# Two 32-column strips of TensorE by turns: the order of the head products in a decoder kernel

## The chip, the cores and the metric

The kernel runs on one core of a Trainium2 chip. The metric is the device time of one launch in microseconds (us). Three runs of the kernel before took 5780.36, 5787.46 and 5790.4 us; the median, 5787.46 us, is the time before.

## The reference

A decoder of four layers works on 32 sequences of 128 tokens with width 128. Each layer has a self-attention, a cross-attention over 77 context tokens and a feed-forward block, each followed by a sum and a layer norm, which makes twelve sublayers. Everything is float32. Three cross-attentions (those of the second, third and fourth layer, called L1X, L2X and L3X) and the self-attention of the fourth layer (L3A) share one form with 16 heads of width 8:

```python
q = split_heads(x @ Wq); k = split_heads(ctx @ Wk); v = split_heads(ctx @ Wv)
p = softmax(scale * q @ k.T + mask)        # 128 queries x 77 keys per head
o = merge_heads(p @ v)                     # 8 columns per head
y = o @ Wo
```

In L3A the keys are the 128 tokens themselves and a term of relative positions is added to the scores. The product p @ v is the one that the change touches.

## The kernel before

The 32 sequences are taken in four steps of eight. In a step the eight sequences are two groups g of four, and all twelve sublayers are done for them before the next step. Each engine has its own instruction list, written out by hand; they meet at semaphores. TensorE takes its list in the order in which it stands.

In L1X, L2X, L3X and L3A the work is cut into 16 units u. A unit is half of one sequence's heads: 8 heads, that is two blocks of 32 columns of the width (i = 0 and 1), each with four heads (r = 0 to 3). A unit passes these stages:

- scores (L1402 in the cross-attentions; L1995 and L1999 in L3A): TensorE multiplies the queries of a block, 32 rows of the array, by the keys, into PSUM banks 0 and 1 or 2 and 3. In L3A four transposes per bank put the position term there first.
- VectorE (DVE) takes the maximum and subtracts it (L1283 to L1292), ScalarE (ACT) takes the exponential (L1254), VectorE the sum and its reciprocal (L1299, L1301), GpSimd (POOL) multiplies (L1314).
- pe_probs_turn (L1222): TensorE transposes the eight 128 x 77 probability tiles into PSUM banks 4 and 5. ScalarE (L1261) and VectorE (L1308) copy them to the buffer PT, one bank each.
- pe_heads (L1239): the head products. The stationary operand is a 77 x 32 slice of v, in which only the 8 columns of head r are not zero; the moving operand is the turned probability tile of that head, 77 x 128. Four products, r = 0 to 3, add up in the 32 partitions c0 to c0+31 of PSUM bank 6 + g. Each product names its strip of the array by tile_position=(0, c0). Strip and target partitions differ between i = 0 and i = 1; the rows of the array are the same.

Each float32 product is two weight loads and two matmuls for TensorE, so the eight head products of a unit are 16 matmul records at L1239, called a burst below. A transpose is one record.

TensorE's list in such a sublayer is, for i from 0 to 18: scores(i), heads(i-3), turn(i-2). VectorE's is less_max(i), sums(i-1), copy of turned(i-2). At i = 5 TensorE also turns the second group's state and makes its queries (L159, L1377), at i = 12 it projects the first group's heads (L1247); at i = 13 and 14 VectorE sums and normalises the first group. Units 13 to 15 have no scores beside them any more.

Before a burst TensorE waits for both copies of the turned tiles. The last matmul of a burst raises c_pv, on which the copies of the next unit wait, and, at units 7 and 15, the copy of the heads.

The self-attention L1A has a head product of its own (L999), with 64-column strips. It already goes from one strip to the other with each product:

```python
for b in range(NB):
    for h in range(2):
        mm = nc.tensor.matmul(ps[64 * h:64 * h + 64, 4, b * P:(b + 1) * P], ...,
                              start=True, stop=True, tile_position=(0, 64 * h))
```

Of the kernel before, what the change touches and what calls it, by code (L numbers as in the profile page):

```python
# [56 lines left out]
def build(nc, dram, cols, out, steps):  # L57

    ctx = ExitStack()
    with ctx:  # L60
# [1165 lines left out]
        def pe_heads(pe, L, u):  # L1226
            m = CB[L]
            nk = m["nk"]
            j, half = divmod(u, 2)
            g, b = divmod(j, NB)  # L1230
            pe.wait_ge(c_ea.sem, c_ea[L, u])
            pe.wait_ge(c_ed.sem, c_ed[L, u])
            if u % 8 == 0:
                pe.wait_ge(c_vc.sem, c_vc[L, g])
                pe.wait_ge(c_qc.sem, c_qc[L, g])
            for i in range(2):
                c0 = 32 * (2 * half + i)
                for r in range(4):
                    mm = nc.tensor.matmul(ps[c0:c0 + 32, 6 + g, b * P:(b + 1) * P],  # L1239
                                          m["v"][g][0:nk, b, r, c0:c0 + 32], m["PT"][0:nk, 4 * i + r, :],  # L1240
                                          start=(r == 0), stop=(r == 3), tile_position=(0, c0))
            mm.then_inc(c_pv.sem, 1)
# [144 lines left out]
        def pe_context(L):  # L1387
            m = CB[L]

            def run(pe):  # L1390
# [18 lines left out]
                for i in range(16 + 3):  # L1409
                    if i == 5:  # L1410
                        pe_context_queries(pe, L, 1)
                    if i < 16:
                        scores(i)
                    if 0 <= i - 3:
                        pe_heads(pe, L, i - 3)
                    if 0 <= i - 2 < 16:
                        pe_probs_turn(pe, L, i - 2)
                    if i == 12:
                        pe_project_heads(pe, L, 0)
                    if i == 17 and L == L2X:  # L1420
                        pe_l2f_route(pe, 0)
                    if i == 16 and L == L1X:
                        pe_turn_state(pe, L1X, 0)
                    if i == 17 and L == L1X:
                        pe_l1f_gate_up(pe, 0)
# [531 lines left out]
        def pe_l3a(pe):  # L1957
# [45 lines left out]
            for i in range(16 + 3):  # L2003
                if i < 16:
                    scores(i)
                if 0 <= i - 3:
                    pe_heads(pe, L3A, i - 3)
                if 0 <= i - 2 < 16:
                    pe_probs_turn(pe, L3A, i - 2)
                if i == 12:  # L2010
                    pe_project_heads(pe, L3A, 0)
                if i == 16:
                    pe.wait_ge(c_sub.sem, c_sub[L3A, 15])
                    pe_context_part(pe, L3X, "k")
                if i == 17:
                    pe_context_queries(pe, L3X, 0)
                    pe_context_part(pe, L3X, "v")
# [776 lines left out]
```

## Time and profile before

| | |
|---|---|
| runs | 5780.36, 5787.46, 5790.4 us; median 5787.46 |
| span of the profiled execution | 5793.5 us |
| mean granted clock of TensorE | 0.836 of full speed |
| TensorE matmul busy | 4923.2 us, 85% of the span |
| VectorE busy | 2980.6 us, 51% |
| ScalarE busy | 1939.1 us, 33% |
| GpSimd busy | 1042.2 us, 18% |
| L1239 in the costliest groups | 353 us (w_even) as its largest part, 4096 matmul records in all |

The profile is of one execution. For it the span is the only time that is given; it lies 6 us above the median of the runs. PE is TensorE's matmul, PEld its weight load. A group is a line, an engine and an operation; "idle before" is the time in which the engine stood still just ahead of it, with the one that ended the wait. The granted clock is 1.0 at 2.4 GHz and 0.5 at 1.2 GHz. Matmul durations are those of single instructions, from start to end of their results; they overlap in the array, so a burst lasts much less than the sum of them. TensorE's busy time is the time in which at least one is under way.

### The profile page before, as it was taken

The numbers are of one execution on the slowest core, as the hardware profiler recorded it, in microseconds if no ns is written. First come the engines' busy times: TensorE is split into PE (matmuls) and PEld (weight loads), VectorE is DVE, ScalarE is ACT, GpSimd is POOL, SyncE is SP. The second block draws the span as 40 slices with busy tenths as digits, with TensorE's granted clock in tenths as the row PEclk, the third lists the DMA queues.
The fourth block names the chain that finished last, engine by engine and source line by source line (L and its number), as shares of the span: only waits on it lengthen the run. The fifth ranks groups of instructions, "written<-read, shape, count | busy, mean of one in ns | idle before, by whom it ended". The sixth has DMA issues, their size and how long they took to land. (4 is left out here: it accounts for less than half of the span.)

```text
span 5793.5 us, 57753 instructions
## 1 busy us (share of the span) xinstructions
PE 4923.2 (85%) x20360; PEld 2783.9 (48%) x20360; DVE 2980.6 (51%) x6224; ACT 1939.1 (33%) x3508; POOL 1042.2 (18%) x876
## 2 busy tenths in 40 slices
PE   6888899989688889998968888998886888899888
PEld 4445454653444545465344454445534455545553
DVE  5555443763555544376355554446535555534643
ACT  4242222336324222233632422222364242223235
POOL 2021100213202110021320211002222021100222
PEclk8896879969799777996879987898597998789869
DMA  2000100000100010000010001000001000100000
GB/s 75 1 3 24 52 5 2 1 16 0 51 1 3 24 52 5 2 1 15 0 51 1 3 24 52 5 2 16 1 1 50 1 3 24 52 5 2 16 1 4
DMA packets 20876, 93.08 MB, mean 16 GB/s; under 512 B 5228, under 2 KB 14444, under 8 KB 17796
## 3 DMA queue, kind: packets, MB, share of 16 engines
q1 hardware_dynamic: 20580, 89.26, 4.1%
q8 instruction: 170, 2.79, 0.2%
q14 instruction: 126, 1.03, 0.1%
HBM read 87.16 MB, written 2.10 MB: 15 GB/s over the span
## 5 line engine op out<-in xcount | busy, mean ns | idle before, releaser
L1314 POOL TENSOR_TENSOR arena<-arena 128x616 f32<-128x616 f32 (+1 forms) x256 | 355.0, 1387 | 1189.2 <-DVE arena L1301 1188.8
L1254 ACT ACTIVATE arena<-arena 128x616 f32<-128x616 f32 (+1 forms) x256 | 205.2, 802 | 930.7 <-DVE arena L1288 481.2
L1222 PE MATMUL ps<-const,arena 128*77 128x128 f32 (+1 forms) x2048 | 422.0, 373 | 69.1 <-POOL arena L1314 69.1
L210 POOL TENSOR_SCALAR rstd_e<-mean_var 128x4 f32<-128x4 f32 x120 | 27.4, 228 | 2467.8 <-DVE mean_var L176 2467.8
L1923 DVE TENSOR_TENSOR arena<-ps,arena 128x512 f32<-128x512 f32 x256 | 176.5, 691 | 468.7 <-ACT arena L1873 468.7
L1222 PEld LDWEIGHTS ps<-const,arena 128*77 128x77 f32 (+1 forms) x2048 | 340.1, 207 | 153.6 <-POOL arena L1314 82.2
L1239 PE MATMUL ps<-arena,w_even 77*32 77x128 f32 (+1 forms) x2560 | 352.9, 355 | 50.8 <-DVE arena L1308 50.4
L1873 ACT ACTIVATE arena<-ps 128x512 f32<-128x512 f32 x288 | 172.0, 597 | 607.9 <-PE ps L1821 607.9
L1239 PEld LDWEIGHTS ps<-arena,w_even 77*32 77x32 f32 (+1 forms) x2560 | 264.3, 141 | 190.8 <-ACT arena L1261 87.1
L2263 PE MATMUL ps<-w_even,w_odd 128*128 128x512 f32 x640 | 321.6, 649 | 26.9 <-issue 26.9
L1308 DVE COPY arena<-ps 77x512 f32<-77x512 f32 (+1 forms) x256 | 174.5, 682 | 270.2 <-PE ps L1222 270.1
L1820 PE MATMUL ps<-xT,w_even 128*128 128x512 f32 x576 | 308.9, 618 | 3.1 <-DVE arena L1910 3.1
L1827 PE MATMUL ps<-arena,w_even 128*128 128x512 f32 x576 | 295.0, 594 | 7.0 <-DVE arena L1923 4.7
L745 PE MATMUL ps<-xT,w_even 128*128 128x512 f32 (+1 forms) x544 | 269.2, 618 | 0.4
L1821 PE MATMUL ps<-arena,w_even 128*128 128x512 f32 x512 | 266.3, 602 | 0.0
L1261 ACT ACTIVATE arena<-ps 77x512 f32<-77x512 f32 (+1 forms) x256 | 151.0, 590 | 328.7 <-PE ps L1222 328.5
L1402 PE MATMUL ps<-arena 32*128 32x308 f32 x768 | 211.3, 663 | 41.8 <-DVE arena L1288 25.2
L199 DVE TENSOR_TENSOR y_tok<-ps,x_tok 128x512 f32<-128x512 f32 x72 | 49.4, 686 | 357.3 <-PE ps L683 265.5
L1299 DVE TENSOR_REDUCE arena<-arena 128x8 f32<-128x616 f32 (+1 forms) x256 | 228.2, 892 | 0.5
L1559 PE MATMUL ps<-arena,w_odd 128*128 128x512 f32 x512 | 220.4, 592 | 0.0
L2263 PEld LDWEIGHTS ps<-w_even,w_odd 128*128 128x128 f32 x640 | 125.2, 205 | 186.9 <-issue 179.2
L2467 DVE SCALAR_TENSOR_TENSOR arena<-ps,arena 128x512 f32<-128x512 f32 x48 | 33.2, 692 | 343.8 <-ACT arena L2352 342.9
(383 smaller groups left out, 9365.4 us busy)
## 6 DMA issues: line engine op xcount, KB each, us to landing
w_even<-in_w SPq DMA_DIRECT2D x4, 6916.0 KB, 19.2
w_even<-in_w SPq DMA_DIRECT2D x4, 3313.5 KB, 10.9
w_odd<-in_w SPq DMA_DIRECT2D x4, 2824.5 KB, 9.4
w_odd<-in_w SPq DMA_DIRECT2D x4, 2095.0 KB, 8.2
w_odd<-in_w SPq DMA_DIRECT2D x4, 2048.0 KB, 15.2
x_in<-in_x SPq DMA_DIRECT2D x10, 256.0 KB, 2.8
w_odd<-in_w SPq DMA_DIRECT2D x4, 577.0 KB, 3.6
w<-in_w SPq DMA_DIRECT2D x1, 2050.0 KB, 10.7
```

The costliest lines, as they stand in the source:

```text
L745: mm = nc.tensor.matmul(ps[0:rows, k + i % 2, :], lhsT, xT[g][:, :], start=True, stop=True)
L1222: mm = nc.tensor.transpose(ps[0:nk, 4 + h // 4, (h % 4) * P:(h % 4 + 1) * P], m["P"][u % 3][:, h, :], ident)
L1239: mm = nc.tensor.matmul(ps[c0:c0 + 32, 6 + g, b * P:(b + 1) * P], m["v"][g][0:nk, b, r, c0:c0 + 32], m["PT"][0:nk, 4 * i + r, :], start=(r ...
L1254: nc.scalar.activation(p, p, ACT.Exp, scale=scale).then_inc(c_exp.sem, 1)
L1299: nc.vector.tensor_reduce(m["sum"][u % 3], m["P"][u % 3], AX.X, ALU.add)
L1314: nc.gpsimd.tensor_tensor(m["P"][u % 3], m["P"][u % 3], bcast(m["sum"][u % 3], m["nk"]), ALU.mult)\
L1402: mm = nc.tensor.matmul(ps[:, 2 * (u % 2) + i, 0:4 * KC], m["q"][g][r:r + 32, b * P:(b + 1) * P], m["k"][g][r:r + 32, b, :, :], start=True ...
L1559: mm = nc.tensor.matmul(bank(4 + n % 2), W(L1F, w)[:, k * T + c * P:k * T + (c + 1) * P], src[g][:, k, :], start=(k == 0), stop=(k == 3))
L1820: nc.tensor.matmul(bank(i % 2), w1, xT[g][:, :], start=True, stop=True)
L1821: nc.tensor.matmul(bank(2 + i % 2), w3, x3, start=True, stop=True).then_inc(e_gu.sem, 1)
L1827: nc.tensor.matmul(bank(6 + g), w, e_h[i % 2], start=(n == 0), stop=(n == 35)).then_inc(e_down.sem, 1)
L2263: nc.tensor.matmul(o, W(L3F, "ew2")[:, p * 384 + m * P:p * 384 + (m + 1) * P], i_hm[g][4 * (j - 1) + p], start=(p == 0), stop=False)
```

## The change

In pe_heads the two loops are exchanged. Before, the four products of strip i = 0 are issued, then the four of strip i = 1. After, the products alternate: r = 0 of both strips, r = 1 of both, and so on. The number of products, their operands, the sums in each strip and their order, and the last instruction of the burst (r = 3 of i = 1) stay the same; L3A, L1X, L2X and L3X all call this function.

```diff
-            for i in range(2):
-                c0 = 32 * (2 * half + i)
-                for r in range(4):
+            for r in range(4):
+                for i in range(2):
+                    c0 = 32 * (2 * half + i)
                     mm = nc.tensor.matmul(ps[c0:c0 + 32, 6 + g, b * P:(b + 1) * P],
                                           m["v"][g][0:nk, b, r, c0:c0 + 32], m["PT"][0:nk, 4 * i + r, :],
                                           start=(r == 0), stop=(r == 3), tile_position=(0, c0))
```

TensorE's instructions in L1X, one turn of the loop, in its list; the eight products of a burst stand in one row, since a row names shapes and not partitions:

```order
L1402 MATMUL ps<-arena0 128x308 x2
L1239 MATMUL ps<-arena0,w_even 32x128 x8
L1222 MATMUL ps<-const,arena0 77x128 x8
L159 MATMUL ps<-const,x_tok1 128x128 x4
L1377 MATMUL ps<-xT1,w_even 128x512
```

These rows are the same before and after. What moves is inside the row of eight. With a for strip i = 0 and b for i = 1 it was a0 a1 a2 a3 b0 b1 b2 b3 and is a0 b0 a1 b1 a2 b2 a3 b3. The two rows L159 and L1377 stand in the turn i = 5 alone.

TensorE's instructions in L3A, one turn:

```order
L1995 MATMUL ps<-const,arena1 128x128 x4
L1999 MATMUL ps<-w_odd,w_even 128x512
L1995 MATMUL ps<-const,arena1 128x128 x4
L1999 MATMUL ps<-w_odd,w_even 128x512
L1239 MATMUL ps<-arena1,w_even 32x128 x8
L1222 MATMUL ps<-const,arena0 128x128 x8
```

Here too nothing moves but the order within the burst of L1239. The lists of the other engines and of the DMA queues are unchanged.

## Rows read from the trace of the kernel before

**Rows 1.** Page, parts 1 and 4: busy time, and the last-ending chain by engine and line.
```profile
PE 4923.2 (85%) x20360; PEld 2783.9 (48%) x20360; DVE 2980.6 (51%) x6224; ACT 1939.1 (33%) x3508; POOL 1042.2 (18%) x876
...
PE ps L1239 2%; PE ps L1222 1%; PE ps L745 1%; PE ps L2263 1%; PE ps L1402 1%; PE ps L1999 1%; PE ps L755 0%; PE ps L2215 0%; POOL rstd L212 0%; PE ps L974 0%; PE ps L949 0%; PE ps L999 0%; DVE x_tok L182 0%; PE ps L1007 0%; PE ps L1995 0%
```
**Rows 2.** Page, part 5: the copy ahead of the bursts (busy, mean ns | idle before).
```profile
L1308 DVE COPY arena<-ps 77x512 f32<-77x512 f32 (+1 forms) x256 | 174.5, 682 | 270.2 <-PE ps L1222 270.1
```
**Rows 3.** Timeline of PE, L1X of step 1: start us, us, engine, line, operation.
```profile
500.27 1.40 PE L1402 MATMUL ps<-arena 32*128 32x308 f32 x4
501.60 2.78 PE L1239 MATMUL ps<-arena,w_even 77*32 77x128 f32 x16
504.31 1.99 PE L1222 MATMUL ps<-const,arena 128*77 128x128 f32 x8
506.23 1.40 PE L1402 MATMUL ps<-arena 32*128 32x308 f32 x4
```
**Rows 4.** Windows on L1239, one burst in three: us, PE (records touched), PEclk, DMA.
```profile
501.59:502.44 0.85, 0.84 (x4) 0.50 0.00 0
502.44:503.30 0.86, 0.86 (x10) 0.50 0.00 0
503.30:504.15 0.85, 0.85 (x8) 0.50 0.00 0
```
**Rows 5.** Timeline of PE, L1A: its head products, at either clock.
```profile
333.31 1.97 PE L999 MATMUL ps<-arena 128*64 128x128 f32 x16
...
339.86 1.09 PE L999 MATMUL ps<-arena 128*64 128x128 f32 x16
```
**Rows 6.** Windows on L1239 by stage: us, PE busy (records) PEld busy (records), PEclk.
```profile
461.00:556.00 95.00, 39.14 (x256) 28.57 (x256) 0.60 0.00 1
687.00:783.00 96.00, 39.25 (x256) 28.70 (x256) 0.57 0.02 10
1060.00:1157.00 97.00, 26.55 (x256) 21.34 (x256) 0.92 0.00 1
1171.00:1268.00 97.00, 40.53 (x256) 29.40 (x256) 0.57 0.00 1
1915.00:2002.00 87.00, 36.17 (x256) 27.02 (x256) 0.66 0.00 1
2134.00:2234.00 100.00, 41.80 (x256) 30.12 (x256) 0.53 0.02 10
...
3366.00:3443.00 77.00, 30.78 (x256) 23.99 (x256) 0.78 0.00 1
...
sum 1509.00, PE 569.86 PEld 425.66; mean PE 35.62 PEld 26.60
```
**Rows 7.** Timeline of DVE, L3X of step 1, one turn.
```profile
1221.89 0.69 DVE L1308 COPY arena<-ps 77x512 f32<-77x512 f32 x1 [1.03 <-PE ps L1222]
...
1223.23 0.86 DVE L1283 SCALAR_TENSOR_TENSOR arena<-ps,arena 128x308 f32<-128x308 f32 x2 [0.65 <-PE ps L1402]
```
**Rows 8.** Timeline of PE, L1X of step 3, at the full clock.
```profile
3402.18 1.50 PE L1239 MATMUL ps<-arena,w_even 77*32 77x128 f32 x16 [0.15 <-DVE arena L1308]
```
**Rows 9.** Windows of one turn each, L1X, L3X, L3A: busy PE, PEld, DVE, ACT, POOL.
```profile
3401.35:3404.75 3.40, 3.25 (x30) 2.43 (x30) 3.19 (x5) 1.31 (x2) 1.14 (x1) 1.00 0.00 0
1215.93:1221.89 5.96, 5.96 (x30) 4.10 (x30) 4.05 (x8) 1.31 (x3) 1.22 (x2) 0.50 0.00 1
1108.55:1114.15 5.60, 5.60 (x37) 3.55 (x37) 4.36 (x5) 2.12 (x3) 1.89 (x2) 1.00 0.00 0
```
**Rows 10.** Timeline, L3A of step 1: a burst, and VectorE's wait for the scores.
```profile
1108.44 1.53 PE L1239 MATMUL ps<-arena 128*32 128x128 f32 x16
1108.55 1.22 DVE L1290 TENSOR_REDUCE arena<-ps 128x8 f32<-128x1024 f32 x1 [1.09 <-PE ps L1999]
```
**Rows 11.** Timeline of PE, L3X of step 1, a late unit.
```profile
1259.25 2.75 PE L1239 MATMUL ps<-arena,w_even 77*32 77x128 f32 x16 [0.87 <-DVE arena L1308]
```
**Rows 12.** Timeline of PE, L1X, around turn 5: steps 1 and 3.
```profile
477.79 2.78 PE L1239 MATMUL ps<-arena,w_even 77*32 77x128 f32 x16
...
3387.96 1.50 PE L1239 MATMUL ps<-arena,w_even 77*32 77x128 f32 x16 [0.15 <-DVE arena L1308]
```

## The prediction

> **What bounds the kernel now.** I read the page's busy times first, then the chain of waits by line. The reader is to see in them that TensorE is busy for 85% of the span and that no other engine passes 51%, and that L1239, the line of the change, is the first line of the chain [rows 1]. The share of 2% that the chain gives it is too small for a sum, since most of TensorE's time there is not put down to a line; so the sum has to come from the stages.
>
> Next I read the timeline of one turn of the loop. In L1X of step 1 scores, heads and turn follow each other without a gap; a turn lasts 506.23 - 500.27 = 5.96 us, of which the burst of L1239 holds 2.78 us [rows 3]. That is at 1.2 GHz. VectorE waits in this loop: over the whole span its 77-row copies of the turned tiles wait 270.1 us for TensorE [rows 2]. The stages differ, and the windows by stage tell how: the granted clock averages 0.53 to 0.60 in L2X, L3X and the L1X of step 1, 0.66 and 0.78 in the later L1X, and 0.92 in L3A [rows 6].
>
> Then, who sets the pace at each clock:
> - L1X, L2X and L3X at 1.2 GHz: TensorE. In a turn of L3X it is busy for all of the 5.96 us and VectorE for 4.05 [rows 9]; VectorE waits 1.03 us for the turned tiles and 0.65 us for the scores [rows 7].
> - L1X at 2.4 GHz: VectorE. It is busy for 3.19 of 3.40 us, in pieces with short drains between [rows 9], and the burst waits 0.15 us for its copy [rows 8].
> - L3A at 2.4 GHz: TensorE. It is busy for all of 5.60 us, VectorE for 4.36 [rows 9], with a wait of 1.09 us for the scores [rows 10].
>
> **What the new order does to a burst.** The 16 records of a burst are two chains of eight. Eight records of the same 128 columns in L1222 take 1.99 us at 1.2 GHz [rows 3]. Of a record's end some 0.42 us is the last one's own duration, so records follow each other every (1.99 - 0.42) / 7 = 0.22 us. Sixteen one after the other would take 15 x 0.22 + 0.42 = 3.8 us; the burst takes 2.78. So the strips overlap already, for part of the time. The windows show which part: in the first third 4 records are touched, in the second 10, in the last 8 (those that straddle a border count twice) [rows 4]. Strip b begins when strip a is half done, both run side by side, and b finishes alone. I read this as a look-ahead of a few instructions: with a's four products in front, b's first one is reached late. If products alternate, b is reached at once, and eight records' time is enough for all sixteen.
>
> The trace has this case. L999 alternates between two 64-column strips, with the same 128 moving columns and the same 16 records: 1.97 us at 1.2 GHz and 1.09 us at 2.4 GHz [rows 5]. Its strips are wider and its rows more, so a burst of L1239 should not be slower. That gives the prices:
> - at 1.2 GHz: 2.78 - 1.97 = 0.81 us less. The upper end is eight records alone, 1.99 as in L1222 with its wider weights, or 7 x 0.213 + 0.42 = 1.91 us at the pitch of (2.56 us of window over 12 pitches) = 0.213 [rows 4], so 0.87 us less. The lower end is nothing, if 32-column strips behaved otherwise than 64-column ones.
> - at 2.4 GHz: 1.53 - 1.09 = 0.44 us less in L3A [rows 10, 5], 1.50 - 1.09 = 0.41 in L1X [rows 8].
> I take 0.81 and 0.44, the nearest rows.
>
> The Trainium skill says otherwise in one place: "TensorE: Matmul & The Clock Gate", Part 3, holds that weight loads overlap running matmuls only where the row group differs. Here both strips use the same rows, and by that rule alternation would hide nothing. The rows of L999, all of whose products share all rows, do not agree with it. The price by the rule is the first rival's.
>
> **How many bursts, and which are on the path.** The 256 bursts have 569.86 us of PE busy time in the 16 stages [rows 6]. A fast burst has 1.50 to 1.53 us, say 1.52; a slow one 2.78, that is 1.26 more. Slow bursts: (569.86 - 256 x 1.52) / 1.26 = 143. By stage in the same way (a stage is 16 bursts, 24.3 us if all are fast): L1X has 11.8, 9.4, 5.1 and 5.1 (its fourth stage reads like its third, as the later stages of L2X and L3X read like those shown), 31 together; L2X has 11.9 and three times 13.9, L3X four times 12.9, together 105; L3A the other 7.
>
> - Slow bursts: a turn is then nothing but TensorE's own work, so the whole 0.81 is on the path. That holds for late units too, which have no scores beside them: burst, turn and copy follow in a line, and TensorE waits 0.87 us for the copy [rows 11], which only starts sooner. What is late next in a turn is VectorE: its wait of 1.03 us for the turned tiles [rows 7] shrinks to 0.22 and does not vanish. The wait of 0.65 for the scores stays, as the copy and the scores both come sooner by the same time. 143 x 0.81 = 116 us.
> - Fast bursts of L3A: 64 - 7 = 57. VectorE's slack of 1.09 us covers 0.44. Around turns 12 to 15, where first the projection and then the next sublayer's state is waited for, I leave three per stage out. 45 x 0.44 = 20 us.
> - Fast bursts of L1X, L2X and L3X: 256 - 143 - 57 = 56. VectorE sets the pace; the work that hides the gain is its 3.19 us per turn. Only the last unit or two of a stage, where burst, copy and projection stand in a line, give back: some 9 x 0.41 = 4 us. The other 47 give nothing.
>
> The sum is 116 + 20 + 4 = 140 us against the span of 5793.5, so 5653.5. The median lies 6 us below the span; for the median I get 5787.5 - 140 = 5647.5, say 5648 us.
>
> No other engine's list changes, no DMA, no wait. The copy of the next unit waits on the burst's last matmul, which comes sooner. Both strips add into one PSUM bank, in different partitions; that they do so together is nothing new, since the middle third of a burst does it now [rows 4].
>
> **What the clock can do to the sum.** In the loop at 1.2 GHz TensorE is never idle [rows 9], and the clock of L2X still averages 0.53 [rows 6]. Around turn 5 the same list is slow in step 1 (2.78 us a burst) and fast from then on in step 3 (1.50) [rows 12]; so the rise hangs on when things fall, and shorter bursts move that. Per turn of L1X the clock is worth 5.96 - 0.81 - 3.40 = 1.75 us afterwards. The L1X stages last 95, 87, 77 and 77 us now, 336 together [rows 6]. I expect about as many slow units as before, spread otherwise, and put the term at nothing; both ends are rivals.
>
> **The rivals.**
> 1. The strips of 32 columns don't load side by side (the skill's rule), or the look-ahead stops at each change of strip. Against it stand L999 and the overlap in the middle third. Time: no change, 5787. If only half of the overlap came, 70 us would, 5717. Chance 0.03.
> 2. L1X loses its fast turns: the array does the same work per turn while the turn of VectorE is no shorter, so TensorE stands idle longer (3.25 of 3.40 us are busy now [rows 9], about 2.8 then). All four stages would be like the first, 95 us less 11.8 x 0.81 = 85, together 340 us. Now they have 336; the sum counts on 336 - 31 x 0.81 - 2 = 309. So 31 us of the 140 go, and the time is 5679. Chance 0.15.
> 3. L1X is fast from turn 5 on in every step: four times 77 - 5.1 x 0.81 = 73, so 292 instead of 309, 17 us more gained; some units of L2X and L3X that rise too give up to 20 more. Time 5615 to 5630. Chance 0.13.
> 4. VectorE, not TensorE, paces the slow turns of L2X and L3X, say since the copy was ready by a hair only: half of 105 x 0.81 = 85 us is lost, 5690. Against it is the slack of 1.03. Chance 0.03.
> 5. Slower than before: the granted clock of L3A falls. It runs at 0.92 on average [rows 6] with TensorE busy throughout; a turn is 5.60 us, and 5.16 after. At 1.2 GHz TensorE's 5.16 would be some 10.3. It decides from about 116 / 5 = 23 units on, counting the rest of the gain; all 57 units would cost 57 x 5 = 285 us, so 5787 - 120 + 285 = 5950. Against it: TensorE has no idle time in this loop and gets none, since VectorE needs 4.36 us of 5.16. Chance 0.02.
>
> **The numbers.** The forecast, 5648 us with its own range of 5630 to 5668, has 0.64. Rivals 2 and 4 lie above it, at 5668 to 5695, rival 3 below, at 5610 to 5630. The range from 5608 to 5690 takes in the forecast's own range, rivals 2, 3 and the edge of 4, with room for two of them at half strength. What a measurement of this kernel tells from no change is about 0.2%, 12 us. Faster has 0.95 (all but rivals 1 and 5), no change 0.03, slower 0.02.
>
> **What would show it.** In the changed profile: L1239's sixteen records take 1.9 to 2.0 us at 1.2 GHz and about 1.1 at 2.4 (if 2.78 stays, rival 1). A slow turn of L1X, L2X or L3X takes 5.15 us, and VectorE's wait before L1308 is 0.2 us. A fast turn of L1X stays at 3.4 us with a longer idle time on TensorE. A turn of L3A takes 5.16, VectorE's wait before L1290 0.65 us. L1239's busy time over the stages goes from 570 to about 143 x 1.97 + 113 x 1.09 = 405 us. The prediction is wrong in its mechanism if bursts are short and turns are not; it is wrong in its size if turns are as said and the clock of the stages in L1X has moved from 0.60, 0.66, 0.78, 0.78.

## The result

The changed kernel takes 5600.16 us (median of 5598.32, 5599.96, 5600.35 and 5606.52), the kernel before 5788.57 us in the same runs. The ratio is 0.966 with a 95% interval of 0.9624 to 0.9696: 188 us less. The forecast was 5648 us, with a range from 5608 to 5690. The sign was right, and so was what the new order does to a burst; the time lies below the range.

The profile after has a span of 5596.7 us, 196.8 us less than the 5793.5 us of before. The page's first part, with the busy time of each engine, answers to [rows 1]:

```profile
PE 4691.9 (84%) x20360; PEld 2608.5 (47%) x20360; DVE 2974.4 (53%) x6224; ACT 1933.6 (35%) x3508; POOL 1042.5 (19%) x876
```

TensorE lost 231 us of matmul busy time with the same number of instructions; VectorE, ScalarE and GpSimd lost next to nothing. The page's line for the copies ahead of the bursts (busy, mean ns | idle before) answers to [rows 2]. Their wait for TensorE has halved, from 270 to 131 us:

```profile
L1308 DVE COPY arena<-ps 77x512 f32<-77x512 f32 (+1 forms) x256 | 173.5, 678 | 132.5 <-PE ps L1222 131.4
```

The timeline of TensorE at the start of L1X in step 1 (start us, us, engine, line, operation, in brackets the idle time before) answers to [rows 3, 12]:

```profile
465.08 1.92 PE L1239 MATMUL ps<-arena,w_even 77*32 77x128 f32 x16
466.93 1.99 PE L1222 MATMUL ps<-const,arena 128*77 128x128 f32 x8
468.71 1.06 PE L159 MATMUL ps<-const,x_tok 128*128 128x128 f32 x4
470.46 1.13 PE L1377 MATMUL ps<-xT,w_even 128*128 128x512 f32 x2 [0.69 <-ACT xT L167]
471.52 0.79 PE L1402 MATMUL ps<-arena 32*128 32x308 f32 x4
472.23 1.07 PE L1239 MATMUL ps<-arena,w_even 77*32 77x128 f32 x16
```

And the same place in the kernel before:

```profile
468.22 2.78 PE L1239 MATMUL ps<-arena,w_even 77*32 77x128 f32 x16
470.93 1.99 PE L1222 MATMUL ps<-const,arena 128*77 128x128 f32 x8
472.71 1.06 PE L159 MATMUL ps<-const,x_tok 128*128 128x128 f32 x4
474.46 2.07 PE L1377 MATMUL ps<-xT,w_even 128*128 128x512 f32 x2 [0.69 <-ACT xT L167]
```

Two things are to be seen. A burst takes 1.92 us at 1.2 GHz for 2.78, and 1.07 us at 2.4 GHz. And the query product L1377, which is no part of the change, takes 1.13 us instead of 2.07: the granted clock rose just before it, about when the full-width transposes L1222 and L159 ended. Before it did not, and the next bursts took 2.78 us. The profile after shows this rise at turn 5 in all twelve cross-attention stages (the burst of unit 2, the first behind L159 and L1377, is fast in each); the profile before in none of the twelve. The fast burst of step 3 in [rows 12] is that of unit 3: the one of unit 2 took 2.78 us there too, and the rise came a turn later.

The windows on L1239 by stage (us, PE busy, PEld busy, granted clock), one step and the L1X of steps 2 and 3, answer to [rows 6]:

```profile
459.00:525.00 66.00, 20.50 (x256) 15.43 (x256) 0.84 0.00 1
658.00:739.00 81.00, 25.64 (x256) 18.60 (x256) 0.65 0.01 4
1020.00:1111.00 91.00, 19.64 (x256) 14.66 (x256) 0.89 0.00 1
1125.00:1205.00 80.00, 26.19 (x256) 19.30 (x256) 0.63 0.00 1
1855.00:1922.00 67.00, 20.50 (x256) 15.40 (x256) 0.84 0.01 1
...
3250.00:3318.00 68.00, 20.50 (x256) 15.41 (x256) 0.84 0.00 1
```

L1X went from clocks of 0.60, 0.66 and 0.78 to 0.84 in every step, L2X from 0.57 and 0.53 to 0.65 and 0.64, L3X from 0.57 to 0.63. Only L3A, at 0.92 before, is a little lower.

The timeline of VectorE in a slow turn of L2X, and in a turn of L3A, answers to [rows 7, 10]:

```profile
702.98 0.69 DVE L1308 COPY arena<-ps 77x512 f32<-77x512 f32 x1 [0.18 <-PE ps L1222]
...
704.32 0.86 DVE L1283 SCALAR_TENSOR_TENSOR arena<-ps,arena 128x308 f32<-128x308 f32 x2 [0.65 <-PE ps L1402]
```
```profile
1044.30 1.22 DVE L1290 TENSOR_REDUCE arena<-ps 128x8 f32<-128x1024 f32 x1 [0.63 <-PE ps L1999]
```

The wait for the turned tiles shrank from 1.03 to 0.18 us, that in L3A from 1.09 to 0.63; the one for the scores stayed at 0.65. These are the numbers forecast. What is not is how many turns are slow.

**Where the 196.8 us came from.** The starts of the bursts in the timelines give each stage's length from its first burst to its last:

| stage | before, steps 1 to 4 | after, steps 1 to 4 | less | slow bursts before, after |
|---|---|---|---|---|
| L1X | 90.9, 82.9, 73.0, 73.0 | 63.7, 63.6, 63.6, 63.6 | 65 | 34, 16 |
| L2X | 91.4, 94.9, 95.0, 95.0 | 78.7 each | 61 | 54, 40 |
| L3A | 93.0, 93.0, 93.1, 93.0 | 87.9, 87.9, 87.8, 87.8 | 21 | 8, 12 |
| L3X | 92.9 each | 77.3, 77.2, 77.2, 77.3 | 63 | 52, 44 |

The stages give 210 us. Some 13 us go back between them; the stretch from L2X's last burst to L3A's first alone went from 282.0 to 284.2 us in each step (slow here means in part or whole at 1.2 GHz; 148 bursts before, 112 after). At the clocks of before, the measured burst lengths give: 143 bursts at 1.2 GHz x (2.78 - 1.92) = 123 us, 45 x (1.53 - 1.07) = 21 us in L3A, 9 x 0.43 = 4 us in the late units, 148 us in all. The other 49 us are what is left. Most of it is the clock's: more turns at 2.4 GHz. It also holds a few us by which fast turns of L1X became shorter, and is net of the 13 us that went back. That split is arithmetic; the stages with and without the rise, below, give a second way to it.

### The profile page after: what moved, and what is told of

Same layout as the page of the kernel before. It is cut to its first block and busy times, and to the rows that moved or that the text cites. A ratio compares the mean times of both kernels' runs of the same rounds, so it can differ in the third digit from the quotient of the medians.

```text
span 5596.7 us, 57753 instructions
## 1 busy us (share of the span) xinstructions
PE 4691.9 (84%) x20360; PEld 2608.5 (47%) x20360; DVE 2974.4 (53%) x6224; ACT 1933.6 (35%) x3508; POOL 1042.5 (19%) x876
## 3 DMA queue, kind: packets, MB, share of 16 engines
q14 instruction: 126, 1.03, 0.1%
## 5 line engine op out<-in xcount | busy, mean ns | idle before, releaser
L1222 PE MATMUL ps<-const,arena 128*77 128x128 f32 (+1 forms) x2048 | 401.6, 359 | 60.4 <-POOL arena L1314 60.4
L1222 PEld LDWEIGHTS ps<-const,arena 128*77 128x77 f32 (+1 forms) x2048 | 321.4, 197 | 141.0 <-POOL arena L1314 80.5
L1239 PE MATMUL ps<-arena,w_even 77*32 77x128 f32 (+1 forms) x2560 | 225.5, 333 | 79.9 <-DVE arena L1308 78.4
L1239 PEld LDWEIGHTS ps<-arena,w_even 77*32 77x32 f32 (+1 forms) x2560 | 166.3, 132 | 185.1 <-ACT arena L1261 111.5
L1402 PE MATMUL ps<-arena 32*128 32x308 f32 x768 | 187.1, 595 | 41.8 <-DVE arena L1288 25.3
```

The lines of the kernel that those rows point to most:

```text
L1222: mm = nc.tensor.transpose(ps[0:nk, 4 + h // 4, (h % 4) * P:(h % 4 + 1) * P], m["P"][u % 3][:, h, :], ident)
L1402: mm = nc.tensor.matmul(ps[:, 2 * (u % 2) + i, 0:4 * KC], m["q"][g][r:r + 32, b * P:(b + 1) * P], m["k"][g][r:r + 32, b, :, :], start=True ...
```

## The experiments

Each kernel was timed beside runs of the kernel before. Those differ more from chip to chip and from run to run (from 5766 to 5825 us over all) than the prediction supposed, so the ratio is what compares. In the first four kernels the burst's line is L1238, one line higher. Stage lengths and counts of slow bursts are those of one profiled execution of each kernel.

**Alternation in L3A alone.**

```diff
-            for r in range(4):
-                for i in range(2):
+            for r, i in ([(r, i) for r in range(4) for i in range(2)] if L == L3A else
+                         [(r, i) for i in range(2) for r in range(4)]):
```

> The strips alternate in L3A alone; the three cross-attentions keep the order of before. Theory A (the surplus over the predicted 140 us comes from the granted clock of the cross-attentions, which rises around turn 5 when bursts there are short): L3A's four stages give 5 us each, the cross-attentions keep 12 to 14 slow bursts per L2X and L3X stage, and the time is 5768 us, give or take 10. Theory B (a short burst is worth more than priced wherever it stands, by something later in the sublayer): 64 of 256 bursts give a quarter of 188 us, 5741.

Measured: 5758.27 us beside 5808.18, ratio 0.9925 (0.9896 to 0.9954), 43 us less. By the total theory B would have it, which gave 47. The profile says otherwise. L3A's four stages are 88.7 us long each, 4.3 less than before. The L3X stages, whose order is that of before, are 87.2 us long for 92.9, 23 us in all. The timeline of the first of them:

```profile
1148.20 2.78 PE L1238 MATMUL ps<-arena,w_even 77*32 77x128 f32 x16
1154.15 2.78 PE L1238 MATMUL ps<-arena,w_even 77*32 77x128 f32 x16
1161.95 1.53 PE L1238 MATMUL ps<-arena,w_even 77*32 77x128 f32 x16
1166.39 1.50 PE L1238 MATMUL ps<-arena,w_even 77*32 77x128 f32 x16 [1.16 <-DVE arena L1307]
1171.44 1.50 PE L1238 MATMUL ps<-arena,w_even 77*32 77x128 f32 x16 [1.80 <-DVE arena L1307]
1176.11 2.77 PE L1238 MATMUL ps<-arena,w_even 77*32 77x128 f32 x16
```

Bursts of 2.78 us in the old order, and behind turn 5 three of 1.50 to 1.53 us, which the kernel before has in no L3X. Nothing in L3X was changed; what differs is L3A ahead of it, which is shorter and has short bursts. L1X, as little changed, lasts 73.0, 82.9, 66.3 and 73.0 us, 25 us less in all. So the rise does not need short bursts, and theory B's total was met by accident: only 17 us come from the sublayer that was changed. Theory A's 20 us fit that part; its total is off by 23 us, since it left the clock of the other stages alone.

**Alternation in the cross-attentions alone.** The same edit with L != L3A.

> The strips alternate in L1X, L2X and L3X alone; L3A keeps the order of before. Theory A: the gain of the change less L3A's 21 us, so 5788 - 167 = 5621 us, and the L1X stages run slow in 4 bursts of 16. Theory B: three quarters of 188, 5647 us.

Measured: 5616.74 us, ratio 0.9671 (0.9643 to 0.9699). L2X and L3X are as long as with the whole change (78.7 and 77.3 us), L1X lasts 81.0, 63.6, 63.6 and 63.6 us, L3A 90.7. By the ratio that is 190 us less, where theory A had 167 and theory B 141. A is the nearer of the two, and the stages of L2X and L3X bear it out; its four slow bursts per L1X stage came in three of the four, and the first has 13. L3A, whose order is that of before, lasts 2.3 us a stage less than before, 9 of the 23 us that theory A lacks; the rest was not traced to a stage. This ratio cannot be told from the whole change's.

**Strips by turns in pairs and in threes.**

```diff
+            for r, i in [(0, 0), (1, 0), (0, 1), (1, 1), (2, 0), (3, 0), (2, 1), (3, 1)]:   # pairs
+            for r, i in [(0, 0), (1, 0), (2, 0), (0, 1), (1, 1), (2, 1), (3, 0), (3, 1)]:   # threes
```

> The order a0 a1 b0 b1 a2 a3 b2 b3 in all four sublayers. In the kernel before strip b began together with the fifth of a's eight records, with three of a's records still ahead of it. Theory C (TensorE reaches past up to three waiting records of one strip): b's first record finds three ahead, starts at once, and a burst lasts 1.92 us at 1.2 GHz and 1.07 at 2.4, as with full alternation; time 5600 us. Theory D (only strict alternation of products hides the second strip, each change of strip waits for the product ahead): a burst lasts some 2.3 us at 1.2 GHz and 1.3 at 2.4, and the time is 5650 us or more.

> The order a0 a1 a2 b0 b1 b2 a3 b3 in all four sublayers. Theory C: six of a's records stand ahead of b, so b starts with a's third record, 0.43 us late at 1.2 GHz: a burst lasts 1.92 + 0.43 = 2.35 us at 1.2 GHz and 1.07 + 0.22 = 1.29 at 2.4. Half of the bursts' gain remains; the clock goes its own way, so the time is 5690 us within 30. Theory D: as long as before, 2.78 and 1.50 us, and 5788 us.

Timeline of TensorE in L1X of step 1, bursts of units 1 and 2, with pairs:

```profile
464.60 1.93 PE L1238 MATMUL ps<-arena,w_even 77*32 77x128 f32 x16
471.76 1.09 PE L1238 MATMUL ps<-arena,w_even 77*32 77x128 f32 x16
```

and with threes:

```profile
464.86 2.35 PE L1238 MATMUL ps<-arena,w_even 77*32 77x128 f32 x16
472.05 1.31 PE L1238 MATMUL ps<-arena,w_even 77*32 77x128 f32 x16
```

Theory C gave 1.92 and 1.07 for pairs, 2.35 and 1.29 for threes; theory D is out. The single records say the same. At 1.2 GHz strip a's records start every 0.21 us. Strip b's first one starts 0.86 us behind a's first in the kernel before, 0.43 us behind it with threes, and 0.01 us behind it with pairs: each time with three of a's records in the list between it and the newest one of a that has started. So TensorE doesn't start its records strictly in the order of its list, as the description of the kernel has it; it reaches past three waiting records of a strip for the next strip's, and in these runs not past more. The times are 5615.68 us (ratio 0.9672, 0.9637 to 0.9708) and 5618.52 (0.9677, 0.964 to 0.9715). For threes that is 70 us less than expected: a burst is 0.43 us longer than with the whole change, and the total is nearly the same, with 116 slow bursts for 112 and stages of 65.8 (L1X), 80.8 to 89.1 (L2X), 89.3 (L3A) and 79.1 to 82.3 us (L3X). With pairs, the bursts are as short as with the change, one of the L1X stages lasts 81.1 us instead of 63.6, and three of the L3X stages have no rise behind turn 5 and last 79.8 instead of 77.3. The total answers to burst length and to clock together and separates neither.

**A shift of the cross-attention stages.** Three or five small products more ahead of a stage's first scores, in the kernel after and in the kernel before; they are overwritten.

```diff
+                    for _ in range(3 if u == 0 else 0):          # or 5
+                        nc.tensor.matmul(ps[:, 0, 0:2 * KC], m["q"][g][0:32, 0:P], m["k"][g][0:32, 0, 0:2, :],
+                                         start=True, stop=True, tile_position=(0, 0))
                     for i in range(2):
```

> The changed kernel; before the first scores of each of the twelve cross-attention stages TensorE repeats a small product three times (two keys' blocks of the first head block, into a PSUM place that the scores overwrite). At 1.2 GHz this is some 3 x 0.51 = 1.5 us a stage, 18 us in all, and nothing else changes. Theory A (whether the granted clock rises around turn 5 hangs on when the stage falls): a shift of 1.5 us can take the rise away; an L1X stage then lasts some 81 us instead of 64, and the total is 5618 us plus 10 to 100. Theory E (short bursts bring the rise at any time, since TensorE does its work denser): 5618 us, and every L1X stage lasts 65.

> As before with five repeats, some 2.6 us a stage, 31 us in all. Theory A: the rise at turn 5 is kept or lost by stage, not as with three repeats; 5631 us plus 0 to 100. Theory E: 5631 us, L1X stages 66 us.

> The kernel before with three repeats before the first scores of each cross-attention stage: 18 us of added work. Theory A: a shift can bring the rise at turn 5 to the long bursts too; then L1X stages last 74 us instead of 82 to 91, units of L2X and L3X run fast, and the time is less than 5788 + 18 = 5806 us, perhaps less than 5788, although work was only added. Theory E: 5806 us, give or take the few per mille by which runs of before differ.

> The kernel before with five repeats, 31 us of added work. Theory A: a time away from 5788 + 31 = 5819 us by tens of us, and a number of slow bursts other than the 143 of before. Theory E: 5819 us and 143 slow bursts.

| kernel | time, ratio (interval) | L1X stages, us | fast behind turn 5, of 12 |
|---|---|---|---|
| before | 5788.57 | 90.9, 82.9, 73.0, 73.0 | 0 |
| before, 3 more | 5770.46, 0.9943 (0.9906 to 0.998) | 73.0, 90.9, 90.9, 73.0 | 4 |
| before, 5 more | 5765.09, 0.995 (0.9906 to 0.9993) | 82.8, 82.9, 73.0, 66.3 | 4 |
| after | 5600.16, 0.966 (0.9624 to 0.9696) | 63.7, 63.6, 63.6, 63.6 | 12 |
| after, 3 more | 5632.2, 0.9689 (0.9607 to 0.977) | 63.6, 63.6, 63.5, 81.1 | 7 |
| after, 5 more | 5630.43, 0.9686 (0.9572 to 0.9799) | 81.1, 81.1, 63.5, 81.1 | 6 |

The windows on L1239 for the four L1X stages of the kernel after with three more show the two cases side by side; the instructions of the four are the same:

```profile
458.00:524.00 66.00, 20.13 (x254) 15.31 (x256) 0.84 0.00 1
1861.00:1928.00 67.00, 20.50 (x256) 15.43 (x256) 0.84 0.00 1
3264.00:3331.00 67.00, 20.49 (x256) 15.44 (x256) 0.84 0.00 1
4665.00:4749.00 84.00, 27.74 (x256) 19.46 (x256) 0.60 0.00 1
```

17.5 us hang on whether the clock rises at turn 5, 0.84 against 0.60. The added products ran at 2.4 GHz, where TensorE waits for VectorE soon after, and took 12.3 us of its busy time in all with three and 19.2 us with five, not the 18 and 31 us expected. The kernel before became faster by half a per cent, an interval just clear of no change, though only work was added; its first L2X stage now has a granted clock of 0.63 and 36.72 us of PE busy time in L1239, where it had 0.57 and 39.25 [rows 6]:

```profile
664.00:757.00 93.00, 36.72 (x256) 27.27 (x256) 0.63 0.03 10
```

Theory E falls on both sides: the kernel before took less time with added work, and short bursts don't bring the rise at any time, since it is missing behind turn 5 in five and six of the twelve stages after. That the added products are what took it away is not shown. The profiled execution of the five more was one of 5650.88 us, its other run 5609.98, so with the same instructions two executions differ by 41 us; by the ratios' intervals neither kernel can be told from the kernel after; and the rise fails in an L1X stage of two kernels without added products as well (81.0 us with the cross-attentions alone, 81.1 with pairs).

Stages without the rise give the second way to the clock's part. L1X takes 90.9 us before and 81.1 after, L2X 95.0 and 84.4, L3X 92.9 and 79.8 (with pairs). These differences, 9.8, 10.6 and 13.1 us, are close to what 12, 14 and 13 slow bursts cost at 0.86 us (10.3, 12.0 and 11.2), and four of each with L3A's 21 us make 155 us. Of the stages' 210 us some 55 are left for the clock, before the 13 us that went back between stages. So the clock's part is real, but in part luck of which stages get the rise.

**Score products as neighbours.** In L3A, behind the transposes of both banks.

```diff
                 for i in range(2):
                     out = bank(2 * (u % 2) + i)
                     for r in range(4):
                         nc.tensor.matmul(out[:, r * P:(r + 1) * P], R["S"]..., ident, is_transpose=True, ...)
+                for i in range(2):
+                    out = bank(2 * (u % 2) + i)
                     p = 32 * (2 * half + i)
                     mm = nc.tensor.matmul(out, R["q"]..., R["k"]..., start=False, stop=True, tile_position=(p, 0), ...)
```

> The changed kernel, and in L3A the score products of the two blocks (L1999), which use different 32-row strips and different banks, stand next to each other behind the transposes of both banks instead of one behind each bank's. Theory C says that products on different strips run side by side as soon as they are neighbours in the list. Then a unit's two products last as one, 0.86 us less of TensorE's 5.15 us per turn; VectorE's slack of 0.63 us is the cap, so a turn of L3A takes 4.5 to 4.6 us, 6 to 7 us less a stage, 25 us in all: 5575 us against the changed kernel's 5600. Theory D (the gain of the change was peculiar to column strips that add into one bank): nothing, 5600 us.

Measured: 5557.13 us, ratio 0.9601 (0.957 to 0.9631). The four records of a unit's two score products (here L2001) take 1.13 us, as two of them did in the kernel after (L1999):

```profile
1044.15 1.04 PE L1995 MATMUL ps<-const,arena 128*128 128x128 f32 x8
1045.12 1.13 PE L2001 MATMUL ps<-w_odd,w_even 32*128 32x512 f32 x4
```
```profile
1047.70 0.66 PE L1995 MATMUL ps<-const,arena 128*128 128x128 f32 x4
1048.28 1.12 PE L1999 MATMUL ps<-w_odd,w_even 32*128 32x512 f32 x2
```

L3A is 81.1 us long for 87.8, 27 us in four steps as theory C had it. The total is 18 us less than expected, for another 8.6 us a step came between L2X's last burst and L3A's first. They are in the first units' scores, which the expectation had left out: from the first L1995 to the first burst it is 24.5 us in the kernel after and 15.8 here. The granted clock over that stretch is 0.54 in the kernel after and 0.78 here, so the order and the clock share in them; no run parts the two. L3X lost 4 us a stage: it has the rise behind turn 5 in none of its four stages.

**Some transposes twice, in L2X and L3X.**

```diff
+            for h in range(2 if L in (L2X, L3X) else 0):
+                nc.tensor.transpose(ps[0:nk, 4, h * P:(h + 1) * P], m["P"][u % 3][:, h, :], ident)
             for h in range(8):
```

> The kernel of the run before with two of the eight transposes of the probabilities done twice in L2X and L3X: 0.43 us more full-width work per unit at 1.2 GHz, 0.21 at 2.4. Theory A (in these stages the clock stays low or falls because TensorE's work is thin, and what raises it is dense full-width work): more units run at 2.4 GHz, where VectorE hides the added work, and the eight stages together take 0 to 30 us less than in the run before. Theory E (the clock doesn't answer to such work): some 84 slow bursts times 0.43, so 36 us more.

Measured: 5529.28 us, ratio 0.954 (0.9494 to 0.9586), the fastest of all the kernels here. The work added is 256 transposes, and the time is 28 us less than that of the kernel without them; the bursts wholly at 1.2 GHz went from 119 to 75, L3X from 81 to 75.4 us a stage, L2X from 79 or 82 to 75.2, 82.4, 72.5 and 82.4. The two ratios' intervals overlap by a little, but both kernels ran on the same chip, the one in 5528 to 5531 us and the other in 5554 to 5576. With more full-width work more turns ran at 2.4 GHz, as theory A has it and theory E has not. A rival stands beside theory A: the added work also moves everything behind it, and in the kernel before small products alone went with more fast bursts. No run adds the same time with thin work inside the turns, so that it is the full width that counts is not shown.

**The same in L1X too.** The condition is now L != L3A.

> The kernel of the run before with two transposes of the probabilities done twice in L1X too, so in all three cross-attentions. Theory A: an L1X stage lasts 64 us, of which ten units run at 2.4 GHz already with VectorE setting the pace; the added turns cost the 4 slow units 0.43 us each and the end of the stage little, so 1 to 3 us a stage more unless the rise comes earlier: 5529 to 5541 us. Theory E: the same added work costs 16 x 0.3 = 5 us in each of four stages, 5550 us.

Measured: 5544.41 us, ratio 0.956 (0.9513 to 0.9607): no gain over the kernel before it. Three of four L1X stages still take 63.3 us, the first takes 69.4. Theory A's upper end was 5541, theory E's number 5550; the total doesn't part them. The stages do: all four of L1X together take 5 us more, where theory E had 5 us for each, and the larger loss stands in L2X, whose list is the same and whose stages last 82.3 or 82.4 us each for 75.2, 82.4, 72.5 and 82.4.

**L1A's strips in groups.** The two loops over b and h at L999 exchanged, in the kernel after.

> The changed kernel with L1A's head products (L999) put back in groups: four products of one 64-column strip, then four of the other. Theory C: sixteen records again with four products ahead of the second strip, so the burst goes from 1.09 to 1.5 us at 2.4 GHz, as L1239 had it before; 64 bursts, TensorE on the path in L1A, so 64 x 0.41 = 26 us more, 5626 us. Theory D' (64-column strips load side by side in any order): 1.09 us still, 5600 us.

Measured: 5624.74 us, ratio 0.9705 (0.9658 to 0.9751), 25 us more than the kernel after. The timeline answers to [rows 5], at 1.2 and 2.4 GHz:

```profile
333.62 2.61 PE L999 MATMUL ps<-arena 128*64 128x128 f32 x16
340.81 1.58 PE L999 MATMUL ps<-arena 128*64 128x128 f32 x16
```

1.58 us for 1.09 and 2.61 for 1.97. The effect is the same with 64 columns and all 128 rows: theory C. That the total came out at the 26 us expected is in part luck: L1A's head products span 109.1 us a step for 104.2, 20 us in all, and three L1X stages became 3.3 us longer each, with two more slow bursts.

## Why the prediction was right in kind and wrong in size

- "What the new order does to a burst" was right: eight records' time is enough for sixteen. It took the price from L999, 0.81 and 0.44 us; measured are 0.86 and 0.46. At 1.2 GHz that is the upper end of 0.87 which the prediction worked out and did not take. L999 loads 64 columns a record, L1239 only 32; whether that makes the difference was not tested. This makes 8 us of the 57 us by which the profiled span lies below the forecast span of 5653.5 (by the medians the miss is 48).
- Which bursts are on the path: right. Slow turns went from 5.95 to 5.10 us (5.15 forecast), those of L3A from 5.61 to 5.15 (5.16), VectorE's wait from 1.03 to 0.18 (0.22). Fast turns of L1X gave a little after all: units 3 to 9 follow each other every 3.31 us on average in step 1 after, every 3.50 in step 3 before, since VectorE's copy and its next instruction lie closer; some 1 to 2 us a stage. L1239's busy time went from 569.9 to 369.0 us, where 405 was forecast: short bursts and fewer slow ones.
- The failing step is "I expect about as many slow units as before, spread otherwise, and put the term at nothing". Measured are 148 slow bursts before and 112 after, L1X from 34 to 16, worth most of the other 49 us of span. The prediction had seen that the rise hangs on when things fall; it wrongly took from this that it would come out even. Its [rows 12] show no rise at turn 5 on either side, since they set the burst of unit 2 beside that of unit 3. All stages of a kind turned out alike in all four steps, so the luck was not averaged over twelve stages but drawn for a few patterns.
- Rival 3, the clock's good side, was the case that came, and it was sized too small. The sum gave L1X 27 us and L2X and L3X together 87; they gave 65 and 124, so 38 and 37 more, where rival 3 had 17 and 20. It took 73 us for an L1X stage, the windows' 77 less bursts alone. That window held one more slow turn 5, with its query product at 1.2 GHz; from the burst of unit 1 to that of unit 2 that turn took 9.57 us in step 1 and takes 7.16 now, of which the shorter burst is 0.86 and the clock the rest. Its floor of 5615 us was the edge, and the range stopped 8 us short of the result.
- The rule from the Trainium skill, "TensorE: Matmul & The Clock Gate", Part 3, that weight loads overlap running matmuls only where the row group differs, was rightly put aside: both strips use rows 0 to 76, and their sixteen loads and products take the time of eight.
- The slower rival, L3A falling to 1.2 GHz, stayed out: 0.89 for 0.92, with 12 slow bursts for 8.

What stays open: why the clock rises in one stage and not in another with the same instructions. These runs show that it does, and what it costs, but not what decides it.

## What to carry to other kernels

In these runs products on different strips of the array ran side by side from the start only where at most three records of the first strip still waited ahead of the second strip's first one; with float32, where each product is two records, let neighbours in the list lie on different strips, or alternate in pairs. When TensorE is the pace-setter and its clock changes within a stage, count the slow and fast turns on both sides of a change: here the clock gave a third more on top of the direct gain (49 to 148 us), so give the range room for such a term and don't put it at nothing. Look in the same list for other products on different strips that stand apart: here the scores of L3A were worth another 43 us, part of it by the clock.

## What the runs showed of the hardware

- Adding work made this kernel faster in three runs: three or five small products per stage in the kernel before (0.9943 and 0.995), and 256 doubled transposes (0.9601 to 0.954), each time with more turns at 2.4 GHz in the profiled execution. The first two gains are barely clear of noise.
- TensorE starts a record of the other strip ahead of three waiting ones of the first: 0.01 us behind the burst's first record with pairs, 0.43 us with threes, 0.86 us with fours, at 1.2 GHz.
- A granted clock of 0.5 with TensorE busy without a gap is common here: 16 records of 32 columns and 77 rows, eight transposes and four records of 32 rows follow each other in 5.96 us, and L2X averages 0.53 [rows 6, 9]. The rise at turn 5 came behind two runs of full-width work, L1222 and L159, of 2.8 us together.
